# Four column quadrants for the 64 products of an expert's list, in an audio tower with a routed feed-forward, on one core

## The reference

```python
scores = jax.nn.sigmoid(x @ gate_weight.T)
capacity = math.ceil(n / E * TOP_K)                  # 1000
topk_score, topk_ids = jax.lax.top_k(scores.T, capacity)
xg = x[topk_ids]
gate = jax.nn.silu(jnp.einsum('ecd,efd->ecf', xg, Wg))
up = jnp.einsum('ecd,efd->ecf', xg, Wu)
out = jnp.einsum('ecf,edf->ecd', gate * up, Wd) * topk_score[..., None]
y = jnp.zeros((n, d), x.dtype).at[topk_ids.reshape(-1)].add(out.reshape(-1, d))
```

## Time and profile before

| | us |
|---|---|
| median of 3 runs | 2097.63 (2095.09 to 2100.26) |
| the profiled execution, its own time | 2095.16 |
| span of the profiled execution | 2093.5 |
| TensorE busy | 1937.0 (93%) |
| VectorE busy | 1351.9 (65%) |
| ScalarE busy | 1070.5 (51%) |
| GpSimd busy | 702.5 (34%) |

### The profile page before, as it was taken

One profiled execution on the slowest core, in us unless ns is written; L12 is line 12 of the kernel. 1 busy time (PEld: TensorE's weight loads), 2 busy tenths in 40 slices (PEclk: granted clock), 3 DMA queues, 4 the chain that ended last, 5 costly groups with the idle time before them and its releaser, 6 DMA issues. The chain is left out here.

```text
span 2093.5 us, 46401 instructions
## 1 busy us (share of the span) xinstructions
PE 1937.0 (93%) x13428; PEld 1660.4 (79%) x13428; DVE 1351.9 (65%) x3700; ACT 1070.5 (51%) x2588; POOL 702.5 (34%) x587
## 2 busy tenths in 40 slices
PE   2899999999999999999958899899999999999997
PEld 2788888888888788888747777788888888888886
DVE  2578878878878877877847777454555555555531
ACT  2687887887887887787732221222222222222221
POOL 0022222222222222222210002366566655566653
PEclk9899999999999999999979999999999999999999
DMA  5556656666666666666726333244445444444452
GB/s 153 161 160 173 192 168 172 191 169 173 189 170 173 187 172 173 186 174 173 194 74 162 98 102 97 56 82 88 85 88 98 90 84 78 78 78 81 81 94 20
DMA packets 318048, 272.95 MB, mean 130 GB/s; under 512 B 80732, under 2 KB 305326, under 8 KB 317998
## 3 DMA queue, kind: packets, MB, share of 16 engines
q1 hardware_dynamic: 238878, 235.53, 41.4%
q0 software_dynamic: 70656, 30.65, 9.9%
q10 hardware_dynamic: 8464, 6.15, 0.9%
HBM read 151.25 MB, written 120.54 MB: 130 GB/s over the span
## 5 line engine op out<-in xcount | busy, mean ns | idle before, releaser
L1208 POOL DMA_INDIRECT out<-ff_y,ff_idxs x128 | 261.8, 2045 | 244.7 <-DVE ff_y L1481 187.6
L1263 ACT ACTIVATE ff_sg<-ffp_g 128x500 f32<-128x500 f32 x192 | 112.9, 588 | 397.2 <-PE ffp_g L1593 397.2
L1195 POOL DMA_INDIRECT ff_xg<-xs_d,ff_idxg x128 | 204.3, 1596 | 284.5 <-issue 271.2
L524 ACT ACTIVATE sb_prob<-sb_ssb,sb_mx 125x250 f32<-125x250 f32 x512 | 253.1, 498 | 61.0 <-DVE sb_rinv L614 33.1
L1605 PE MATMUL ffp_d<-ff_wd,ff_wide 128*125 128x192 f32 x1536 | 261.2, 327 | 16.2 <-DVE ff_wide L1468 15.4
L1468 DVE TENSOR_TENSOR ff_wide<-ff_sg,ffp_u 128x500 f32<-128x500 f32 x192 | 129.4, 674 | 222.1 <-PE ffp_u L1593 222.1
L1605 PEld LDWEIGHTS ffp_d<-ff_wd,ff_wide 128*125 128x125 f32 x1536 | 247.8, 188 | 20.0 <-issue 18.4
L1593 PE MATMUL ffp_g<-ff_xsp,ff_wsp 128*128 128x500 f32 x960 | 251.2, 392 | 1.9 <-DVE ff_xsp L1345 1.6
L1593 PE MATMUL ffp_u<-ff_xsp,ff_wsp 128*128 128x500 f32 x960 | 248.9, 389 | 0.0
L822 PE MATMUL ps_qps<-sb_hsp,sb_wsp 128*128 128x250 f32 x1280 | 186.8, 293 | 31.5 <-DVE sb_hsp L728 22.8
L1593 PEld LDWEIGHTS ffp_g<-ff_xsp,ff_wsp 128*128 128x128 f32 x960 | 179.8, 189 | 39.8 <-issue 2.4
(11 more groups left out here) (189 smaller groups left out, 3562.6 us busy)
## 6 DMA issues: line engine op xcount, KB each, us to landing
bias_d<-sb_rsb SPq DMA_DIRECT2D x256, 219.6 KB
sb_bsk<-bias_d SPq DMA_DIRECT2D x256, 218.8 KB
hx_d<-sb_hx SPq DMA_DIRECT2D x32, 336.0 KB
sb_hxl<-hx_d SPq DMA_DIRECT2D x32, 336.0 KB
ff_wd<-WdT SPq DMA_DIRECT2D x16, 576.0 KB, 4.9
xs_d<-sb_xs SPq DMA_DIRECT2D x32, 238.0 KB
bias_d<-sb_rsb SPq DMA_DIRECT2D x256, 25.5 KB
sb_bsk<-bias_d SPq DMA_DIRECT2D x256, 25.4 KB
```

The lines of the kernel that those rows point to most:

```text
L524: a.activation(prob[:, s % 2, t], ssb[:, s % 2, t], ACT.Exp, bias=mx[:, s % 2, t:t + 1], scale=-1.0, accum_out=rs[:, t, s:s + 1]).then_inc ...
L1195: g.indirect_dma_start(xg[:, t], None, xs_d[:, :], bass.IndirectOffsetOnAxis(idxg[:, t:t + 1], 0), bounds_check=last).then_inc(gat, 16)
L1208: g.indirect_dma_start(out_d[:, :], bass.IndirectOffsetOnAxis(idxs[:, t:t + 1], 0), y[:, t], None, bounds_check=last, compute_op=ALU.add). ...
```

## The change

The 64 products of a list go in turn to four PSUM slices (product n to partitions 32 (n mod 4) and up), as four sums of 16 products. `list_out` copies the first sum and adds the other three one after another, each of 32 x 64, and combines the two halves of the total from SBUF. The counts of the semaphore `l_ev` go from 2 to 5 a list.

```diff
+LISTS = 128 // LO
...
-        lst = sb("lst", [LO, LO])
+        lst = sb("lst", [LO, LISTS, 2 * LO])
...
-        kps, lps = kl[:, 0:1], kl[0:LO]
+        kps = kl[:, 0:1]
+        lps = [kl[LO * i:LO * i + LO] for i in range(LISTS)]
...
+        L_CHAIN = LISTS + 1
...
-                wait(sp, l_ev, 2 * e + 2)
+                wait(sp, l_ev, L_CHAIN * (e + 1))
...
-                v.tensor_copy(lst[:], lps[:, 0:LO]).then_inc(l_ev, 1)
-                dve.wait_ge(l_ev, 2 * e + 1)
-                v.scalar_tensor_tensor(out=lsti[:], in0=lps[:, LO:2 * LO], scalar=float(TP), in1=lst[:], op0=ALU.mult, op1=ALU.add).then_inc(l_ev, 1)
+                for i in range(LISTS):
+                    if i == 0:
+                        v.tensor_copy(lst[:, i], lps[i]).then_inc(l_ev, 1)
+                    else:
+                        dve.wait_ge(l_ev, L_CHAIN * e + i)
+                        v.tensor_tensor(lst[:, i], lps[i], lst[:, i - 1], ALU.add).then_inc(l_ev, 1)
+                dve.wait_ge(l_ev, L_CHAIN * e + LISTS)
+                both = lst[:, LISTS - 1]
+                v.scalar_tensor_tensor(out=lsti[:], in0=both[:, LO:2 * LO], scalar=float(TP), in1=both[:, 0:LO], op0=ALU.mult, op1=ALU.add).then_inc(l_ev, 1)
...
-                wait(pe, l_ev, 2 * e)
+                wait(pe, l_ev, L_CHAIN * e)
...
-                        ins = m_(lps, one_hi[:, b, c], val[:, n].rearrange("p a n -> p (a n)"), start=n == 0, stop=n == BLOCKS * SPLIT - 1)
+                        ins = m_(lps[n % LISTS], one_hi[:, b, c], val[:, n].rearrange("p a n -> p (a n)"), start=n < LISTS, stop=n >= BLOCKS * SPLIT - LISTS)
```

## The result

Median 2081.72 us after (2080.76 to 2091.14, 7 runs) against 2097.63 before (2095.09 to 2100.44, 7 runs): ratio 0.9936, 95% interval 0.9922 to 0.9951, or 13.4 us less (10.3 to 16.4); the medians themselves differ by 15.9. Forecast: 2082.4, range 2076 to 2090. The profiled execution has a span of 2080.1 us against 2093.5, at a mean granted clock of 0.985 against 0.984.

What follows compares the result with a forecast made beforehand. Each list was taken as bound by streaming columns through one array quadrant. 14 x 1.39 = 19.4, less 4.3 and 0.3, plus 0.4, gave 15.2 us off the 2097.63 median: 2082.4, 8-in-10 range 2076 to 2090.

Steps and rivals of the forecast that it cites:

- The products: TensorE's 64 list products: quadrants fully overlap, first to last start falls from 1.85 to 0.46 us, 1.39 us less a list.
- Behind the list: TensorE after a list: exposed sequencer work loses 0.36 us in 12 back-jump turns, 0.16 us for lists 2 and 15.
- the 17 queued products: Products queued when the sequencer reaches the loop's end: assumed to cover 124 ns of its 0.7 us after the change.
- the bound that I had named: Worst case behind the list: the sequencer arrives with an empty queue and a back jump costs 0.48 us.
- VectorE: `list_out` grows from two operations to five, 0.40 to 1.18 us, hidden because VectorE waits 0.84 us for products today.
- The gather: GpSimd's gather keeps its place from the list's start; TensorE waits up to 0.5 us, free within 1.12 us idle time.
- The first two lists: Lists 0 and 1, before the loop: 0.4 us gained for both together, as `list_out(0)` ends earlier.
- up to 0.9: Loss if TensorE's clock falls earlier, slowing two more transpose groups before the first expert; left at zero.
- No overlap: Rival: list products keep their distance through a fixed cost each, TensorE gains nothing; 2098 us, chance 0.11.
- Partial overlap: Rival: sequencer or weight loads hold list products to 14.6 ns, 0.92 us gained a list; 10.5 us, 2087; chance 0.15.
- No loss behind the list: Rival: the sequencer's 0.7 us after a list are overlapped some other way; 19.9 us less, 2078; chance 0.09.
- Slower: Rival: changing quadrant drains the array, 0.12 us a product, lists 5.7 us longer; 2178 us, chance 0.05.

Runs made afterwards that it cites:

- e1: Kernel after with four sums kept, but products in blocks of 16 per quadrant instead of in turn: 2092.34 us, ratio 0.9989.
- e2: Kernel after with two sums in two quadrants in turn instead of four: 2084.02 us, ratio 0.9955.
- e9: Kernel after with each list product split into two halves of 32 columns, 128 products over four quadrants: 2101.63 us against 2093.47, one run.
- e5: Kernel after with a list's products moved ahead of the last 24 down products, `list_out` left in place: 2083.65 us, ratio 0.9953.
- e4: Kernel before with the copy of `list_out` done five times instead of once: 2093.76 us, ratio 0.9993.
- e10: Kernel before with each list product split into two halves of 32 columns, 128 products on one quadrant: 2118.78 us against 2093.47, one run.
- e3: Kernel after with the copy and additions of `list_out` done twice, nine VectorE operations instead of five: 2082.15 us, ratio 0.9945.
- e11: Kernel after with the first two `one_hots` steps each cut into four instructions: 2079.94 us, ratio 0.9941.
- e6: Kernel after with list products ahead of the last 24 down products and `list_out` ahead of VectorE's last scaling: 2075.11 us, ratio 0.9899.
- e7: As e6, with the four `one_hots` steps of each turn two units earlier: 2071.34 us, ratio 0.9876.

## Why the prediction was right

**The products: right.** 1.847 us from first to last start became 0.491 (forecast 0.46), 1.36 us a list in place of 1.39, 19.0 us for 14 lists. Full overlap of the quadrants is shown by e1, e2 and e9: as long as the supply keeps up, a quadrant keeps its 29 ns (25 at 32 columns) and the four run beside each other. The rest of 0.03 us is the pace of 8.3 ns in the second half of the list, above the 7.3 reckoned with.

**Behind the list: right in kind, a little too small.** 0.21 to 0.25 us from the last list product to the gate product became 0.66 in ten loop turns (0.83 and 0.71 in the other two), against 0.58. Summed over the 12 back jumps the loss is 5.5 us (forecast 4.3), for lists 2 and 15 0.29 and 0.20 (0.16 each). The mis-sized step is the 17 queued products: at 8.3 ns a product the sequencer no longer gets ahead, and the queue is empty. This is close to the bound that I had named, 0.48 a jump, against 0.46 measured. e5 removes this: its fastest turns are 47.19 - 46.65 = 0.54 us shorter. Together 19.0 - 5.5 - 0.5 = 13.0 us. The trace has 11.8 from list 2 to list 15, and 0.8 behind it, where the last body takes 58.56 us in place of 58.15. The change is not the cause: in the other eleven profiles the last body takes 58.4 to 58.6 us, in e4 and e10 too, which keep the one sum. The profile of before was the odd one.

**VectorE: right.** e1, e3 and e4 show that the longer read-out is hidden, even at nine operations.

**The gather: right that it costs nothing, mis-sized on the way.** I took its place as fixed from the list's start and forecast a wait of up to 0.5 us. It was 0.80 to 1.00 us in eight of the 13 turns (not in nine, as I wrote before e3) and none in the other five. What I missed stood in the trace of before: of its 128 gathers, 28 start inside a `one_hots` step of 2.28 us (27 in the first two steps, one in the fourth) and take 2.1 to 3.2 us, where the median of the others is 1.29. With the first gather in some other place against these steps, the last one takes one of a few places some 1.6 us apart (20.7, 22.3, 23.9 and 25.5 us into the body), one gather step of 1.29 + 0.30 us each. This is why e3's 0.9 us had no price, and why e5 falls in some turns by 1.4 us at once. e11 shows the cause: shorter instructions on VectorE, shorter waits on GpSimd.

The Trainium skill names a lock for it, "SBUF — State Buffer", section "SBUF: two separate sides": VectorE and GpSimd share a pair of ports; a VectorE instruction with two inputs in SBUF (against a GpSimd operation that reads SBUF) or in a two-port mode holds it for its whole length, and the other is blocked. The traces agree: the gathers end 1.2 us after VectorE's step. They also agree that not every VectorE instruction does it: over the thirteen profiles 224 gathers start inside the product of gate and up (`ff_wide`, 0.68 us, one input in PSUM), 171 of them with over 0.2 us of it left, and take 1.28 to 1.33 us. Two inputs in SBUF are not needed, though: 149 start inside the third `one_hots` step (0.7 to 1.2 us, one tensor and a column of scalars) and all end 1.15 or 1.16 us after it (1.33 to 1.58 us); the two-port mode would cover that, but no row shows an instruction's mode. And where the page lets whichever starts first hold the pair, the traces show one direction only: in the twelve profiles with whole steps, 301 of the first two steps start while GpSimd issues an indirect transfer and take 2.28 to 2.32 us, the other 83 take 2.27 to 2.29. That it is this port, and not another thing that such an instruction holds, no run separates.

The remaining cover in the kernel after is at most 0.1 us in these turns, so a further delay of the gather by a step would show, as it does in e5.

**The first two lists: mis-sized.** I forecast -0.4 us. In the two profiled executions it was +2.6 from list 0 to list 2: 1.1 for slower first gathers (29.09 in place of 27.95 us from list 0 to the transposes), 0.9 for the four groups of transposes at the low clock, and 0.5 for the units behind them. The slower gathers are the same effect once more. The first gather and VectorE's second `one_hots` step (for list 1) in their timelines:

```profile
1283.27 3.36 POOL L1198 DMA_INDIRECT ff_xg<-xs_d,ff_idxg  x1 [194.80 <-issue]
```
```profile
1283.09 2.28 DVE L1329 TENSOR_TENSOR ff_one_lo<-ff_lo_all,ff_iota 125x2048 bf16<-125x2048 int32 x1
```

The first gather starts 8.57 us behind list 0, inside that step, and the last one at 23.87. In e5 and e6, whose code is the same up to the first unit, it starts at 8.26 and 8.08, ahead of the step, takes 1.38 us, and the last one starts at 20.39; the transposes come 26.65 and 26.71 us behind list 0, sooner than before. In e7, the same code too, it starts at 8.76 and they come at 28.87. What differs ahead of the gathers is above all the time that the store of list 0 takes to land: 3.97 us in the profile of after, 4.16 in e7, 3.79 and 3.61 in e5 and e6. The change has a share: with list 0 shorter by 1.36 us, the step starts 8.39 us behind it in place of 9.74, so that the first gather can meet it. From list 0 to the first unit it is 37.3 us before, 36.5 in e5 and e6, 39.4 in the profile of after and 39.2 in e7. So my -0.4 was neither kind: -0.8 or +2.

The windows show the granted clock (columns: length, busy time of the five engines, then the clock):

```profile
1302.00:1304.00 2.00, 0.21 (x1) 0.24 (x2) 0.00 (x0) 0.00 (x0) 0.00 (x0) 0.57 0.43 137
...
1306.00:1308.00 2.00, 1.10 (x4) 0.70 (x4) 0.26 (x1) 0.55 (x1) 0.00 (x0) 0.50 0.69 182
```

After TensorE stood idle for 4.04 us the clock had fallen to half, 1.2 GHz, before the first transposes, where the kernel before lost it only behind the second group of them. Four transposes took 1.10 us in place of 0.65. That was my "up to 0.9", left at zero because the work ahead of the fall seemed the same; but the idle time ahead grew. The price goes with the wait for the gathers: from the first transposes to the first unit it is 9.38 us before (0.20 us idle), 9.84 in e5 and e6 (1.60 and 1.67 us idle), 10.28 in e7 (3.83) and 10.29 in the profile of after (4.04). It is no fixed rule: in e3 TensorE waited 1.86 us, and it is 9.39. Against this loss, the part ahead of list 0, which the change leaves alone, was 3.4 us shorter in the profile of after. That part varies by itself: over the thirteen profiles the first product of the shared expert starts between 1094.3 us (e2) and 1100.4 (e9), and that goes with the granted clock of the first 120 us: 0.94 to 0.97 in six of them, that of after included, where it starts at 1096.4 or sooner, and 0.91 to 0.93 in the other seven, with that of before, where it starts at 1097.9 or later. These two nearly cancel. That the total of 13.4 us is close to the sum over the lists, and the difference of the medians (15.9) to the forecast (15.2), is therefore partly luck.

**The rivals.** No overlap is refuted for quadrants in turn (0.49 us), though its floor is real inside one quadrant (e10). Partial overlap (0.92 us a list) is what two quadrants give (e2). No loss behind the list is refuted by the 0.46 us of idle time. Slower is refuted: neighbours on different quadrants start 3 to 4 ns apart. By the Trainium skill, "TensorE: Matmul & The Clock Gate", Part 3, "The mechanism", it is about 4 ns between tiles (its picture has tiles of different rows), and the trace agrees for these tiles of different columns.

**Open.** What stops e9 twice in the lists 2 to 15. What in the supply sets 8.3 ns. Why the landing of list 0's store and the clock in the tower vary between executions.

## What to carry to other kernels

A long chain of short products into a few output partitions is bound by one quadrant's distance from start to start (25 ns at 32 columns, 29 at 64). Give them in turn to quadrants that are free and add the sums later on an engine that waits anyway; whole blocks for each quadrant win little. Then look behind the burst: it runs its queue empty, and a branch that was covered comes to light, so put long products between the two (e5, with e6 so that the read-out moves along). And before you count on slack at a GpSimd gather, look at which long VectorE instructions with all their inputs in SBUF it runs beside: slack comes and goes there in whole steps, and 0.2 us in a store's landing can decide over 2 us.

## What the runs showed of the hardware beyond what I expected

- Weight load and product together can be supplied at 8.3 ns a pair, at 32 and at 64 columns; the first 32 of a list start faster.
- At a border between two quadrants the next one's products start beside the last one's: some seven starts about 15 ns apart in e1.
- With 128 short products in a row the supply stopped twice, for 0.24 and 0.31 us, in fourteen of sixteen lists, weight loads and products alike; with 64 it never did.
- A gather step on GpSimd (1.29 us) that starts beside VectorE's 2.28 us instruction with two SBUF inputs takes up to 3.4 us; beside pieces of 0.6 to 0.7 us at most 1.8. Beside an instruction with an input in PSUM (0.68 us) it keeps its time, and VectorE's steps keep theirs beside it.
